# FFN 2's down product: half of it in two fp32r parts for ten pairs of time steps

## What is computed

```python
# layer 0: a mixture of experts and an expert-choice FFN (not touched)
# layer 1, cond: LSTM;  ffn: h = bit_linear(x, w1); h = silu(depthwise_conv1d(h)); bit_linear(h, w2)
def bit_linear(x, w):                       # act_quant per token, weights in {-1, 0, 1} / scale
    return einsum('bsd,hd->bsh', act_quant(x), weight_quant(w))
# layer 2, cond: h = tanh(h @ Wh + x_t @ Wx + b)
# layer 2, ffn:
    h = einsum('bsd,fd->bsf', x, ternary(W1)) + b1      # 128 -> 512
    h = gelu(h)
    out = einsum('bsf,df->bsd', h, ternary(W2)) + b2    # 512 -> 128: the down product
# layer 3, cond: gate = sigmoid(h @ Wh.T + z_t @ Wz.T + b); h = tanh(h * (1 - alpha) + gate * z_t)
# layer 3, ffn: r = sigmoid(xr @ Wr.T); r * (square(relu(xk @ Wk.T)) @ Wv.T), xr and xk mixed from h and its predecessor
```

## Time and profile before

| | |
|---|---|
| median of 3 runs | 554.63 us (554.04 to 554.67) |
| the profiled execution's own time | 554.63 us |
| its span | 553.3 us |
| TensorE busy | 540.1 us (98%) |
| VectorE busy | 425.7 us (77%) |
| ScalarE busy | 380.6 us (69%) |
| GpSimd busy | 197.8 us (36%) |
| granted TensorE clock | full in every slice |

### The profile page before, as it was taken

How to read it: one execution, slowest core, us unless ns; L and a number is a source line. 1 busy time by engine, 2 the same in 40 slices (tenths; PEclk the granted TensorE clock), 3 DMA queues, 4 the chain that set the end, 5 groups by cost and what they waited for, 6 DMA issues and landing times.

```text
span 553.3 us, 10078 instructions
## 1 busy us (share of the span) xinstructions
PE 540.1 (98%) x3341; PEld 468.0 (85%) x3341; DVE 425.7 (77%) x1026; ACT 380.6 (69%) x857; POOL 197.8 (36%) x186
## 2 busy tenths in 40 slices
PE   8999999999999999999999989999999999999997
PEld 7877888887887899999999877788989999987785
DVE  4987656567659779676856359998999999999866
ACT  4567767758767664454552246888988888888965
POOL 4688788788788402947100000010000000000100
PEclk9999999999999999999999999999999999999999
DMA  8634306512081302021000000122111111112211
GB/s 285 194 152 159 152 1 230 191 56 97 2 305 43 124 10 82 1 73 62 2 1 1 0 1 2 20 39 21 21 20 20 21 31 30 34 38 47 45 52 39
DMA packets 30227, 37.36 MB, mean 68 GB/s; under 512 B 20096, under 2 KB 23648, under 8 KB 29280
## 3 DMA queue, kind: packets, MB, share of 16 engines
q1 hardware_dynamic: 30176, 36.72, 21.2%
HBM read 30.24 MB, written 2.28 MB: 59 GB/s over the span
## 4 chain that ended last, share of the span: by engine, by line
PE 81%; DVE 12%; ACT 4%; issue 2%; POOL 1%; DVEq 0%; ACTq 0%
PE bank L325 11%; PE bank L1248 10%; PE bank L327 10%; PE bank L326 10%; PE bank L1673 4%; PE bank L1759 4%; PE bank L1663 4%; PE bank L1700 3%; PE bank L1701 3%; PE bank L1316 2%; PE bank L1198 1%; PE bank L1748 1%; PE bank L1786 1%; PE bank L409 1%; PE bank L1772 1%
## 5 line engine op out<-in xcount | busy, mean ns | idle before, releaser
L387 POOL TENSOR_TENSOR hidden_low<-hidden,hidden_high 128x512 fp32r<-128x512 f32 x72 | 94.4, 1318 | 24.6 <-ACT hidden_high L372 22.4
L2054 POOL CAST h_high<-h 128x256 fp32r<-128x256 f32 x15 | 6.4, 426 | 197.6 <-ACT h L1865 191.2
L452 ACT ACTIVATE bank<-bank 128x512 f32<-128x512 f32 x56 | 32.6, 583 | 34.5 <-PE bank L327 34.3
L456 DVE TENSOR_TENSOR hidden<-bank,big 128x512 f32<-128x512 f32 x56 | 38.5, 688 | 15.8 <-ACT bank L452 14.6
L372 ACT CAST hidden_high<-hidden 128x512 fp32r<-128x512 f32 x70 | 43.0, 615 | 3.3 <-DVE hidden L456 1.9
L1700 PE MATMUL bank<-taps_high,q1T 128*128 128x512 f32 x94 | 42.9, 457 | 1.0 <-ACT q1T L1828 0.6
L325 PE MATMUL bank<-xin_high,sw_high 128*128 128x256 f32 x128 | 43.9, 343 | 0.0
L1701 PE MATMUL bank<-taps_low,q1T 128*128 128x512 f32 x94 | 37.1, 395 | 0.0
L1382 DVE COPY yT<-bank 128x256 f32<-128x256 f32 x32 | 13.6, 424 | 30.4 <-PE bank L1248 30.4
L1801 ACT ACTIVATE gates_t<-bank,lstm_b_half 128x128 f32<-128x128 f32 x96 | 28.2, 364 | 12.2 <-PE bank L1673 8.8
L1663 PE MATMUL bank<-x,lstm_wx 128*128 128x128 f32 x256 | 34.4, 277 | 1.7 <-ACT gates_t L1801 0.9
(11 more groups left out here) (270 smaller groups left out, 1736.6 us busy)
## 6 DMA issues: line engine op xcount, KB each, us to landing
big<-gates_scratch SPq DMA_DIRECT2D x7, 2048.0 KB, 8.1
w<-in_f_w SPq DMA_DIRECT2D x16, 256.0 KB, 6.2
onehot<-topi_scratch SPq DMA_DIRECT2D x8, 512.0 KB, 4.2
outT<-x SPq DMA_DIRECT2D x15, 128.0 KB, 2.1
xT<-in_xT SPq DMA_DIRECT2D x3, 512.0 KB, 7.4
hidden<-in_ffn_w SPq DMA_DIRECT2D x3, 256.0 KB, 5.2
hidden<-in_conv_w SPq DMA_DIRECT2D x3, 256.0 KB, 4.8
xT<-in_xT SPq DMA_DIRECT2D x2, 256.0 KB, 4.2
```

The source lines that it names most:

```text
L387: pool.tensor_tensor(hidden_hl[u % 3][1][:, :], hidden[u % 3][:, :], hidden_hl[u % 3][0][:, :].bitcast(F32), ALU.subtract).then_inc(s_lo, 1)
L456: dve.tensor_tensor(hidden[u % 3][:, :].rearrange("p (i k) -> p i k", k=P), r_bank[j % 2][:, :].rearrange("p (i k) -> p i k", k=P), gate_r ...
```

## The change

It does the following.

- `down2`: for the pairs v < `SPLIT` = 10, two of the four products (f = 2 and 3) are made in two fp32r parts. ScalarE writes the high part (`split_g_high`), GpSimd subtracts to get the low part (`split_g_low`); the weights are kept as fp32r, in a buffer apart from the raw ones.
- GpSimd's subtraction waits until `conv_next(2 v + SPLIT_STEP)` is done.
- `g2` has a ring of three buffers, and the results of `down2` go to bank 6 beside the leaky cell's, so that `up2` waits for the last gelu and no longer for `new_x3`, and `down2` waits for `new_x3` and for the leaky cell's tanh.
- `m2w` is gone: `scale_y` scales by `m2`, and `new_x2` multiplies by `half_ws2` while it adds.
- The programs of TensorE, ScalarE and VectorE are in a new order in ramp, loop and drain. In the loop `down2`, the leaky cell and the mix stand one turn later.

```diff
-            g2 = sb1("g2", [P, HT, 2, N])
+            g2 = sb1("g2", [P, 3, HT, 2, N])
+            g2_high, g2_low = sb1("g2_high", [P, 2, 2, 2, N], F32R), sb1("g2_low", [P, 2, 2, 2, N], F32R)
...
+            SPLIT, SPLIT_STEP = 10, 10
+            RING = 3
...
             def bank_down(v):
-                return (bank[3] if v <= PAIRS else bank[0])[:, 0:width(v) * P].rearrange("p (s n) -> p s n", s=width(v))
+                dst = bank[6][:, 2 * P:4 * P] if v < PAIRS else (bank[3] if v == PAIRS else bank[0])[:, 0:P]
+                return dst.rearrange("p (s n) -> p s n", s=width(v))
...
             def down2(v):
                 if has_block(v):
                     pe.wait_ge(c_g2[0], v + 1)
-                    pe.wait_ge(c_g2[1], v + 1)
+                    if v < SPLIT:
+                        pe.wait_ge(c_glow, v + 1)
+                    else:
+                        pe.wait_ge(c_g2[1], v + 1)
+                    if v == 0:
+                        pe.wait_ge(c_to, EARLY)
+                    elif v < PAIRS:
+                        pe.wait_ge(c_x3, v)
+                        pe.wait_ge(c_g3, 2 * v)
                     for f in range(HT):
-                        mm = pe.matmul(bank_down(v), ffn2_w2[:, f, :], part(g2[:, f, :, :], v),
-                                       start=(f == 0), stop=(f == HT - 1))
+                        if v < SPLIT and f >= 2:
+                            pe.matmul(bank_down(v), ffn2_w2[:, f, :], g2_high[:, v % 2, f - 2, :, :], start=False, stop=False)
+                            mm = pe.matmul(bank_down(v), ffn2_w2[:, f, :], g2_low[:, v % 2, f - 2, :, :],
+                                           start=False, stop=(f == HT - 1))
+                        else:
+                            mm = pe.matmul(bank_down(v), ffn2_w2[:, f, :].bitcast(F32), part(g2[:, ring(v), f, :, :], v),
+                                           start=(f == 0), stop=(f == HT - 1))
                     mm.then_inc(c_down, 1)
...
+            def split_g_high(v):
+                if 0 <= v < SPLIT:
+                    act.wait_ge(c_g2[1], v + 1)
+                    if v >= 2:
+                        act.wait_ge(c_down, v - 1)
+                    act.copy(g2_high[:, v % 2, :, :, :], g2[:, ring(v), 2:HT, :, :]).then_inc(c_ghigh, 1)
...
                     dve.wait_ge(c_m2, p + 1)
-                    dve.tensor_scalar(m2w[:, 2 * p:2 * p + 2], m2[:, 2 * p:2 * p + 2], half_ws2[:, 0:1], None, ALU.mult)
...
                     dve.wait_ge(c_yT, t + 1)
-                    dve.tensor_tensor(x1[:, t, :], x1[:, t, :], ps_yT, ALU.add).then_inc(c_x2, 1)
+                    dve.scalar_tensor_tensor(x1[:, t, :], ps_yT, half_ws2[:, 0:1], x1[:, t, :], ALU.mult, ALU.add).then_inc(c_x2, 1)
...
+            def split_g_low(v):
+                if 0 <= v < SPLIT:
+                    pool.wait_ge(c_ghigh, v + 1)
+                    if v >= 2:
+                        pool.wait_ge(c_down, v - 1)
+                    if 2 * v + SPLIT_STEP < T:
+                        pool.wait_ge(c_conv, 3 * (2 * v + SPLIT_STEP))
+                    pool.tensor_tensor(g2_low[:, v % 2, :, :, :], g2[:, ring(v), 2:HT, :, :], g2_high[:, v % 2, :, :, :].bitcast(F32),
+                                       ALU.subtract).then_inc(c_glow, 1)
...
-            FILL, TURNS = 8, 18
+            FILL, TURNS = 9, 18
...
-                for p in range(PAIRS):
+                for p in range(PAIRS + 1):
                     split_h2(p)
+                    split_g_low(p - 1)
```

More of the change, by code:

```diff
@@ new lines, in pe_program @@
+                gate_h(13)
+                up_tap(10, 0)
+                up2(1, 0)
+                up_tap(10, 1)
+                turn_y(4)
+                turn_h(12)
+                up_tap(10, 2)
+                rnn(4)
+                gate_x(14)
+                up_tap(11, 0)
+                down1(5)
+                turn_h(13)
+                gate_h(14)
+                down2(0)
+                turn_y(5)
+                up_tap(11, 1)
+                up2(1, 1)
+                rnn(5)
@@ L2201, in pe_program @@
+                gate_x(15)
+                turn_q1(12)
+                turn_q1(13)
+                down1(6)
+                gate_h(15)
+                turn_y(6)
+                up_tap(11, 2)
+                up_tap(12, 0)
+                up2(2, 0)
+                turn_h(14)
+                leaky(0)
+                up_tap(12, 1)
+                rnn(6)
+                up_tap(12, 2)
+                gate_x(16)
+                for q in range(FILL, TURNS):
                     up_tap(2 * (q - 3) + 1, 0)
@@ new lines, in pe_program @@
+                    turn_y(2 * (q - 5))
+                    up_tap(2 * (q - 2), 0)
+                    turn_h(2 * (q - 1))
+                    leaky(2 * (q - 8))
+                    up_tap(2 * (q - 2), 1)
+                    rnn(2 * (q - 5))
+                    up_tap(2 * (q - 2), 2)
+                    gate_x(2 * q)
+                    up2(q - 6, 0)
+                mix_products(7)
+                down1(25)
+                up_tap(31, 0)
+                turn_y(25)
+                leaky(19)
@@ L2597, in dve_program @@
                 new_h(11)
+                conv_next(9)
                 silu(3)
-                new_x2(3)
-                max_hs(3)
                 max_h(5)
                 step_h(5)
-                step_hs(3)
-                inverse_h(5)
+                new_x2(3)
+                inverse_h(5)
+                gate_products(12)
+                new_cell(12)
+                conv_here(9)
+                new_h(12)
+                conv_last(9)
+                max_hs(3)
+                step_hs(3)
@@ new lines, in dve_program @@
+                conv_next(10)
+                inverse_hs(3)
+                new_x2(4)
+                gate_products(13)
+                conv_here(10)
+                new_cell(13)
+                conv_last(10)
+                new_h(13)
+                max_h(6)
+                silu(4)
+                max_hs(4)
+                step_h(6)
+                new_x2(5)
+                inverse_h(6)
+                gate_products(14)
+                new_cell(14)
+                conv_next(11)
@@ L2605, in dve_program @@
+                step_hs(4)
+                new_h(14)
+                inverse_hs(4)
+                conv_here(11)
+                new_x3(0)
+                new_x2(6)
+                conv_last(11)
+                conv_next(12)
+                gate_products(15)
+                new_cell(15)
+                conv_here(12)
+                new_h(15)
+                conv_last(12)
+                gated3(0)
+                leaked3(0)
+                silu(5)
                 for q in range(FILL, TURNS):
-                    mix(q - 10, xr, mu_r, c_xr)
@@ L2638, in dve_program @@
+                    gate_products(2 * (q - 1) + 1)
+                    conv_here(2 * (q - 2))
+                    conv_last(2 * (q - 2))
+                    new_cell(2 * (q - 1) + 1)
+                    gated3(2 * (q - 8))
+                    new_h(2 * (q - 1) + 1)
+                    leaked3(2 * (q - 8))
+                    silu(q - 3)
+                new_x2(25)
+                shift_diff(8)
+                max_hs(14)
+                mix(8, xr, mu_r, c_xr)
                 gated3(19)
-                inverse_hs(13)
```

603 lines of the change are left out of this document (304 added, 299 removed).

## The result

The changed kernel takes **556.47 us** (median of 8 runs, 555.96 to 557.38), the kernel before 554.38 us in the same call (8 runs, 553.97 to 554.87): a ratio of **1.0038**, 95% interval 1.0027 to 1.0049. It is slower by some 2 us, where 551.0 was forecast. The profiled executions agree: the span grew from 553.3 to 554.9 us.

The account below looks back on a forecast made before the run. TensorE was taken to bound the loop, at 13.36 us a turn. The terms -3.9 + 0.5 + 0.3 - 0.5 + 0 = -3.6 took 554.6 to 551.0 us; forecast's own range 549.5 to 552.6 (0.5), 8 in 10: 548.5 to 554.7.

Parts of the forecast that it names:

- The down product: TensorE, pairs' down products: two of four in fp32r parts save 0.39 us a pair, -3.9 us for ten pairs.
- All ten count: End of the ramp to about 490 us: TensorE is the bound there, so all ten pairs' savings count.
- ScalarE's cast: ScalarE, ten casts of the high parts at 0.615 us: the margin stays positive, +0.5 us, at most 4.3.
- VectorE or ScalarE taking over the turn: Rival, loop: the turn ends at 13.15 instead of 12.97 us, some 552.6 to 554.2 us; chance 0.19.
- GpSimd's subtraction: GpSimd, ten subtractions of 1.32 us: beside the convolutions, only `new_cell` may be held by 0.2; +0.3 us in all.
- The catching rival: Rival, VectorE behind `conv_next`: the subtraction holds `gate_products`, up to 1.3 us a pair, 557 to 558 us; chance 0.07.
- `new_x2` and `m2w`: VectorE, two stretches beside the loop: dropping the small instruction gains 0.12 us a pair, roughly -0.5 us.
- The turn's order: Ramp and drain: later `down2`, leaky cell and mix give ramp +1.0, drain -1.0, either way some 2 us; taken as 0.
- The pure chain in the drain: Rival, drain: TensorE's work runs out before the leaky chain, 3.8 us lie open, 554 to 555 us; chance 0.08.
- The signs of being wrong: Loop: steady TensorE waits in the turn, or a mixed f32 and fp32r group above 1.35 us, would refute the forecast.

Follow-up runs that it names:

- e9: The changed kernel with the split for pairs 3 to 9 only: 555.97 us, 1.0017 to the kernel before.
- e2: The changed kernel with the split off, its new order kept, all down products in f32: 558.76 us, 1.0073 to the kernel before.
- e10: The changed kernel without the subtraction's wait for the convolution: 555.67 us, 1.0012 to the kernel before.
- after: The changed kernel itself, its sums taken from the one profiled execution: 556.47 us, 1.0038 to the kernel before.
- e5: The kernel before with the scale alone changed (`m2w` gone, `new_x2` multiplies by `half_ws2`): 554.81 us, 1.0001 to the kernel before.
- e1: The changed kernel's functions (bank 6, ring, scale) with the split off and the lists of the kernel before: 558.43 us, 1.0070 to the kernel before.
- e7: e1 with bank 0 for the down products of pairs 11 to 14, without their wait on `c_g3`: 556.90 us, 1.0036 to the kernel before.
- e6: The changed kernel with bank 0 for the down products of pairs 10 to 14, without their wait on `c_g3`: 556.69 us, 1.0030 to the kernel before.
- e12: The changed kernel, split for pairs 3 to 9, subtraction not waiting for the convolution, last ten microseconds in the order of before: 556.61 us, 1.0044.
- e3: e1 with `down2` half a turn later, no split: 571.72 us, 1.0308 to the kernel before.
- e13: e6 with the drain's lists in the order of the kernel before and the left-over work at their start: 567.48 us, 1.0241 to the kernel before.
- e8: The kernel before, its lists and banks kept, with the first two down products split for pairs 2 to 11: 554.45 us, 0.9992.

## Why the prediction was wrong, point by point

- **The down product, -3.9 for ten pairs.** The price was exact (1.34 us), the count was not. Seven pairs gave their 0.39 (e9's sum is 2.6 us below e2's, 7 x 0.39 = 2.7). The three pairs of the ramp gave 0.6 with the subtraction started at once (e10's sum is 0.6 below e9's, 3 x 0.39 = 1.2) and cost 0.8 as the change makes them (after's sum is 0.8 above e9's). "All ten count" was wrong for the three.
- **ScalarE's cast, +0.5.** It took 0.67 us instead of 0.61, and no wait of TensorE for it shows in the turn. VectorE or ScalarE taking over the turn didn't happen.
- **GpSimd's subtraction, +0.3: mis-sized, by a mechanism I had named.** Started at once, it would have cost 1.4 us less (e10 against after, by the sums). The catching rival put the stall at `gate_products` in the turn, ten times. It came at `gate_products` and `new_cell`, once each, in the ramp, 1.7 us in all. The text used the loop's order to say that `gate_products` starts first, and didn't ask the same of the ramp's list. The Trainium skill (SBUF — State Buffer, "Who interferes with whom") says that whichever of the two starts first keeps the shared port pair; the 1.14 and 1.25 us, which end 0.3 and 0.1 us behind the subtraction, agree.
- **`new_x2` and `m2w`, -0.5.** Nothing that e5 could tell from no change. The stretches where it was booked did not get shorter in e5 (55.0 and 37.5 us ahead of the loop, as before; 61.3 behind it, where it was 60.6).
- **The turn's order, 0: this is the step that failed.** Without the split the order with its bank costs 4.0 us (e2 against e5; 3.1 in the profiled sums: -1.5, -2.1, -0.2, +6.8). I booked ramp +1.0 and drain -1.0, and took 0. The ramp gained 3.6 and the drain lost 6.8, both against my signs. The windows of the two drains, first of e5, then of e2:

```profile
492.93:554.20 61.27, 55.31 (x349) 45.78 (x347) 49.12 (x125) 46.73 (x129) 4.59 (x8) 0.97 0.17 44
488.75:556.90 68.15, 60.42 (x375) 49.78 (x372) 53.13 (x135) 50.18 (x137) 4.94 (x8) 0.97 0.15 40
```

TensorE's busy time in the drain grew by 5.1 us and its idle time by 1.8. So the work that left the ramp did not leave idle time there: the ramp got shorter by it. And in the drain it did not lie in the 5.6 us of room that I had counted (1.5 and 4.1): it came on top. What those gaps of the kernel before wait for fits this: ahead of the last recurrence step mostly the recurrence and FFN 1 (L1865, L1998), behind it FFN 3, as here:

```profile
547.01 0.70 PE L1793 MATMUL bank<-kk,ffn_wv 128*128 128x256 f32 x2 [0.76 <-ACT kk L1905]
548.32 0.46 PE L1786 MATMUL bank<-xr,ffn_wr 128*128 128x128 f32 x2 [0.61 <-DVE o L2038]
```

That moved work could not have filled these gaps under any order is an argument, not shown.

- **The waits of `down2` at bank 6.** That on `c_g3` was in the diff, and the text didn't price it. Under the old order bank, ring and waits cost 3.6 us (e1 against e5), 1.5 to 1.9 of them given back by the late bank (e7). Under the new order the turn shows no such cost (80.0 / 6 = 13.3 us in e2).
- **The pure chain in the drain** (554 to 555, with 0.08) came nearest. Its size was too small: the leaky cell stands not one and a half steps later behind the LSTM but two. When the last gate product starts, the kernel before has made 18 leaky steps and the changed one 16. Two steps of 2.5 us would have given 551.0 + 5.0 = 556.0 us, close to the 556.47. That is partly luck, for the chain isn't pure: TensorE is busy for 59.67 of the 67.85 us, and of the waits that its timeline marks there only one, 0.29 us, is for the leaky cell's state. Nor is 2.5 us a floor: the last leaky products of the changed kernel start 2.3 us apart (541.51, 543.73, 546.01).
- **The signs of being wrong** that the text named, steady waits in the turn or a mixed group above 1.35 us, both stayed away. They watch the loop, and the loss lay outside it.

So the result is +4.0 for the order with its bank, less 1.9 for the split as it was made. What stays open is how the 6.8 us of the drain divide between the depth (any order with `down2` one turn later) and this particular order. e6 and e12 exclude the late bank and the last ten microseconds; the two orders of mine that were to settle it (e3, e13) were bad ones.

## What to carry to other kernels

Price an edit and the reordering that makes room for it as two kernels. Here the edit was worth up to 2.8 us under the new order (e9 against e2) and the reordering with its bank cost 4.0; the edit alone in the old order, for the pairs whose turn is steady, is the fastest version, 1.7 us below the kernel before. A saving per turn counts only in turns that have the loop's shape; look up each of the others in the lists, above all for what GpSimd's new instruction starts beside. And before you count idle time in a drain as room, look up what each gap waits for, and whether the work that you move there is ready then.

## What the runs showed of the hardware

- A VectorE instruction that reads two tensors of SBUF is held until about the end of GpSimd's subtraction when it starts behind it: 1.14 instead of 0.42, 1.25 instead of 0.28, 1.19 instead of 0.34 us. The convolution's instruction, which reads PSUM and one tensor of SBUF, keeps 0.75 beside it. In e8 an instruction with a single small tensor was held too, `step_h` at pair 2, 0.93 us instead of 0.16:

```profile
393.80 1.27 POOL L2079 TENSOR_TENSOR g_low<-g,g_high 128x512 fp32r<-128x512 f32 x1 [8.19 <-ACT g_high L1894]
394.16 0.93 DVE L1955 TENSOR_SCALAR m<-mx 128x2 f32<-128x2 f32 x1
```

- Going from f32 to fp32r within one group of accumulating products has no price that shows: 1.34 us for two f32 products and four fp32r ones.
- The granted clock fell in e13's drain, twice before its end. Windows of e13, before and during each fall:

```profile
508.00:517.00 9.00, 5.81 (x33) 4.51 (x32) 5.78 (x13) 4.87 (x10) 0.70 (x1) 1.00 0.01 2
517.20:520.60 3.40, 2.99 (x9) 2.63 (x10) 0.28 (x1) 1.09 (x4) 0.00 (x0) 0.50 0.46 116
521.00:530.50 9.50, 5.16 (x32) 3.68 (x30) 4.05 (x12) 4.37 (x12) 1.12 (x2) 1.00 0.00 0
530.90:534.30 3.40, 3.18 (x10) 2.76 (x11) 1.87 (x6) 2.04 (x5) 0.00 (x0) 0.51 0.28 65
```

TensorE was busy 65% and 54% of the stretches ahead, and then got half the clock, 1.2 GHz, for 3.4 us each. So a part of e13's 11 us is not the waits' own, at most some 3.4 us by my estimate, half of the two stretches.
